# Self-attention of a four-layer kernel: where the causal mask of the transposed scores is applied, which engine splits q and k, and when constants are filled

## The reference

```python
K = jnp.einsum('bse,hed->bhsd', xk, Wk); V = jnp.einsum('bse,hed->bhsd', xv, Wv); Q = jnp.einsum('bqe,hed->bhqd', xq, Wq)
scores = jnp.einsum('bhqd,bhkd->bhqk', Q, K)
causal = jnp.triu(jnp.ones((xq.shape[1], sk), dtype=bool), k=1)
scores = jnp.where(causal, -jnp.inf, scores)
att = jax.nn.softmax(scores / jnp.sqrt(jnp.asarray(sk, scores.dtype)), axis=-1)
out = jnp.einsum('bhqk,bhkd->bhqd', att, V)
out = out.transpose(0, 2, 1, 3).reshape(out.shape[0], out.shape[2], -1)
return jax.nn.relu(out @ Wo + bo)
a = _layernorm(inputs + a, g1, b1)
```

## Time and profile before

| what | value |
|---|---|
| median of three runs | 3115.39 us |
| time of the profiled execution | 3107.04 us |
| its span, first to last instruction | 3105.3 us |
| mean granted TensorE clock | 0.898 of full speed |
| self_stage, first to last work | 1095.2 to 1972 us of the span |

### The profile page before, as it was taken

How to read it: one execution, slowest core, us unless ns; L and a number is a source line. 1 busy time by engine, 2 the same in 40 slices (tenths; PEclk the granted TensorE clock), 3 DMA queues, 4 the chain that set the end, 5 groups by cost and what they waited for, 6 DMA issues and landing times. The chain is left out here.

```text
span 3105.3 us, 44342 instructions
## 1 busy us (share of the span) xinstructions
PE 2582.5 (83%) x13167; PEld 1491.0 (48%) x13183; DVE 1717.8 (55%) x3471; ACT 1266.5 (41%) x2533; POOL 1165.0 (38%) x1679
## 2 busy tenths in 40 slices
PE   7997999999846658888988988699556887699997
PEld 4554666666523323343443433455333475466664
DVE  5884646555378736657556473488686734312211
ACT  4663435443345514555545556266211233122221
POOL 3666641344446630110201100144551062566663
PEclk9998999999968878999999999899657965799999
DMA  3001000001000031221312210110103061122222
GB/s 120 5 1 58 0 0 1 1 1 41 1 31 0 0 83 36 47 53 46 77 41 57 57 40 17 37 46 28 40 29 109 0 210 63 31 45 45 47 44 31
DMA packets 91525, 125.60 MB, mean 40 GB/s; under 512 B 14216, under 2 KB 68593, under 8 KB 89553
## 3 DMA queue, kind: packets, MB, share of 16 engines
q1 hardware_dynamic: 74416, 104.40, 11.4%
q0 software_dynamic: 16928, 18.93, 3.8%
HBM read 84.19 MB, written 38.83 MB: 40 GB/s over the span
## 5 line engine op out<-in xcount | busy, mean ns | idle before, releaser
L2558 ACT ACTIVATE L2S_pT<-L2S_t_ps 128x512 f32<-128x512 f32 (+3 forms) x768 | 353.8, 490 | 236.7 <-PE L2S_t_ps L2456 126.9
L2637 DVE TENSOR_REDUCE L2S_mx<-L2S_s_ps 128x1 f32<-128x768 f32 (+7 forms) x384 | 347.3, 953 | 110.7 <-PE L2S_s_ps L2435 107.6
L2453 PE MATMUL L2S_t_ps<-L2S_q,L2S_k 98*128 98x512 bf16 (+3 forms) x768 | 252.2, 342 | 40.6 <-ACT L2S_pT L2558 33.1
L2434 PE MATMUL L2S_s_ps<-L2S_k,L2S_q 96*128 96x512 bf16 (+3 forms) x768 | 208.5, 344 | 43.6 <-DVE L2S_mx L2637 32.6
L1034 POOL TENSOR_TENSOR L_prob<-L_prob,L_rc 128x616 f32<-128x616 f32 x128 | 156.7, 1225 | 205.8 <-DVE L_rc L980 205.5
L3092 DVE TENSOR_TENSOR L3B_h<-L3B_si,L3B_u_ps 128x512 f32<-128x512 f32 x71 | 48.9, 688 | 237.7 <-PE L3B_u_ps L3035 216.1
L2740 POOL DMA_DIRECT2D L2S_q<-L2S_mrow x32 | 17.3, 541 | 430.9 <-DVE L2S_mrow L2645 430.9
L2453 PEld LDWEIGHTS L2S_t_ps<-L2S_q,L2S_k 98*128 98x128 bf16 x768 | 75.6, 99 | 191.3 <-ACT L2S_pT L2558 147.4
L2471 PE MATMUL L2S_o_ps<-L2S_pT,L2S_v 128*32 128x512 f32 (+3 forms) x1536 | 166.8, 509 | 0.0
L571 POOL TENSOR_TENSOR L_prob<-L_prob,L_rc 128x616 f32<-128x616 f32 x64 | 77.8, 1215 | 234.9 <-DVE L_rc L524 234.9
L3009 POOL DMA_INDIRECT out<-L3B_y,L3F_rows x71 | 114.8, 1616 | 132.7 <-DVE L3B_y L3098 120.4
(11 more groups left out here) (451 smaller groups left out, 5928.2 us busy)
## 6 DMA issues: line engine op xcount, KB each, us to landing
qk_parts<-L2S_part SPq DMA_DIRECT2D x96, 128.0 KB, 2.3
L2S_q<-qk_parts SPq DMA_DIRECT2D x32, 192.0 KB, 3.4
L2S_k<-qk_parts SPq DMA_DIRECT2D x32, 192.0 KB, 3.5
L2S_q<-qk_parts SPq DMA_DIRECT2D x32, 128.0 KB, 3.2
L2S_k<-qk_parts SPq DMA_DIRECT2D x32, 128.0 KB, 3.2
self_attended<-L2S_att SPq DMA_DIRECT2D x4, 1024.0 KB, 4.2
L_xn<-self_attended SPq DMA_DIRECT2D x8, 512.0 KB, 3.6
context_attended<-L_res SPq DMA_DIRECT2D x8, 512.0 KB, 2.6
```

The source lines that it names most:

```text
L2434: nc.tensor.matmul(o[:, z * 512 + c:z * 512 + e], lhs, k6[0:KR, q % 2, h, c:e], start=True, stop=(e < end))
L2453: mm = nc.tensor.matmul(o[:, lo:512], k6[:, q % 2, j, kt * P:(kt + 1) * P], q6[:, q % 2, j, c * 512 + lo:(c + 1) * 512], start=True, stop= ...
L2558: nc.scalar.activation(pT[:, st % 2, j, lo:512], t_ps[j % 2][:, lo:512], ACT.Exp, scale=SK).then_inc(s["exp_done"], 1)
L2637: nc.vector.tensor_reduce(dst, src, AX.X, ALU.max).then_inc(s["mx_done"], 1)
```

## The change

Four edits, all in `self_stage`:

1. The matmul with `cmaskT` goes, with the tile itself. After the exponential of a diagonal unit POOL selects on the 128 x 128 corner of `pT`: what lies above the diagonal becomes 0 (`affine_select`, in place). `values` of a diagonal step waits for the four selections (`masked`). The mask of the peaks stays on PE.
2. DVE, and no longer POOL, makes the second and third part of q and k, right after the rest.
3. The ones in v are filled by DVE after the first layer norm's work.
4. The ones in `k6` are filled by POOL behind the constants. PE waits for them before its first instruction of the stage, and the next instruction of POOL waits as well.

```diff
+    DIAGONAL = [st for st, (c, kt) in enumerate(STEPS) if kt >= 4 * c]
...
-            pe.wait_ge(s["ones_done"], 1)
+            pe.wait_ge(s["k_ones"], 1)
...
                     o, lo = t_ps[j % 2], low(st)
-                    diagonal = kt >= 4 * c
-                    mm = nc.tensor.matmul(o[:, lo:512], k6[:, q % 2, j, kt * P:(kt + 1) * P], q6[:, q % 2, j, c * 512 + lo:(c + 1) * 512],
-                                          start=True, stop=not diagonal)
-                    if diagonal:
-                        mm = nc.tensor.matmul(o[:, lo:lo + P], identb[:], cmaskT[:], start=False, stop=True)
-                    mm.then_inc(s["t_full"], 1)
+                    nc.tensor.matmul(o[:, lo:512], k6[:, q % 2, j, kt * P:(kt + 1) * P], q6[:, q % 2, j, c * 512 + lo:(c + 1) * 512],
+                                     start=True, stop=True).then_inc(s["t_full"], 1)
...
                     pe.wait_ge(s["exp_done"], 4 * step + 4 + 2)
+                    if st in DIAGONAL:
+                        pe.wait_ge(s["masked"], 4 * (TB * (QUADS * b + q) + DIAGONAL.index(st) + 1))
...
-            nc.vector.memset(v[:], 1.0)
-            nc.vector.memset(k6[KR:MR], 1.0).then_inc(s["ones_done"], 1)
...
+                    if b is None:
+                        nc.vector.memset(v[:], 1.0).then_inc(s["ones_done"], 1)
...
                         dve.wait_ge(s["act_pre"], copies + 3 + 2 * m + f)
-                        dve.wait_ge(s["split_done"], 4 * nb + max(2 * m + f - 1, 0) + 1)
+                        n = 4 * nb + 2 * m + f + 1
+                        dve.wait_ge(s["split_done"], n)
                         nc.vector.tensor_tensor(rest[:, f, :], s_ps[f][:], part[:, f, 0, :], ALU.subtract).then_inc(s["rest_done"], 1)
+                        dve.wait_ge(s["rest_done"], n)
+
+                        if m or b is not None:
+                            dve.wait_ge(s[f"written{f}"], (2 * nb + m) * 96)
+                        nc.vector.tensor_copy(part[:, f, 1, :], rest[:, f, :]).then_inc(s["mid_done"], 1)
+                        dve.wait_ge(s["mid_done"], n)
+                        nc.vector.tensor_tensor(part[:, f, 2, :], rest[:, f, :], part[:, f, 1, :], ALU.subtract).then_inc(s["split_done"], 1)
...
-            nc.gpsimd.memset(cmaskT[:], 0.0)
...
-            pool.sem_inc(s["split_done"], 1)
-            first = 1
-            PER = 6
+            pool.wait_ge(s["const_done"], 1)
+            nc.gpsimd.memset(k6[KR:MR], 1.0).then_inc(s["k_ones"], 1)
+            pool.wait_ge(s["k_ones"], 1)
...
-                        nc.gpsimd.tensor_scalar(part[:, f, 1, :], rest[:, f, :], 1.0, None, ALU.mult).then_inc(s["pool_step"], 1)
-                        pool.wait_ge(s["pool_step"], own + 2 + 2 * m + f)
-                        nc.gpsimd.tensor_tensor(part[:, f, 2, :], rest[:, f, :], part[:, f, 1, :], ALU.subtract).then_inc(s["split_done"], 1)
+                def unit(q, st, j):
+                    if st in DIAGONAL:
+                        pool.wait_ge(s["exp_done"], ((QUADS * b + q) * NS + st) * 4 + j + 3)
                         chip.settle(pool)
+                        edge = pT[:, st % 2, j, low(st):low(st) + P]
+                        nc.gpsimd.affine_select(out=edge, in_=edge, compare_op=ALU.is_ge, fill=0.0, base=0,
+                                                pattern=[[1, P]], channel_multiplier=-1).then_inc(s["masked"], 1)
```

More of the change, by code:

```diff
@@ L2181, in self_stage @@
         xres = behind[:, 2 * S:].rearrange("p (t d) -> p t d", d=D)
-        cmask, cmaskT, identb = sb("cmask", [P, P], BF16), sb("cmaskT", [P, P], BF16), sb("identb", [P, P], BF16)
+        cmask, identb = sb("cmask", [P, P], BF16), sb("identb", [P, P], BF16)
         mx = sb("mx", [P, 2, 4, TB])
@@ L2588, in link @@
                 dve.wait_ge(s["dve_step"], step.up())
-            nc.vector.memset(v[:], 1.0)
-            nc.vector.memset(k6[KR:MR], 1.0).then_inc(s["ones_done"], 1)
             dve.sem_inc(s["mx_done"], 2)
+            dve.sem_inc(s["split_done"], 1)
             dve.sem_inc(s["r_free"], 1)
@@ L2700, in _ @@
             nc.gpsimd.affine_select(out=cmask[:], in_=cmask[:], compare_op=ALU.is_ge, fill=BIG, base=0,
-                                    pattern=[[-1, P]], channel_multiplier=1)
-            nc.gpsimd.affine_select(out=cmaskT[:], in_=cmaskT[:], compare_op=ALU.is_ge, fill=BIG, base=0,
-                                    pattern=[[1, P]], channel_multiplier=-1).then_inc(s["const_done"], 1)
-            pool.sem_inc(s["split_done"], 1)
+                                    pattern=[[-1, P]], channel_multiplier=1).then_inc(s["const_done"], 1)
+            pool.wait_ge(s["const_done"], 1)
+            nc.gpsimd.memset(k6[KR:MR], 1.0).then_inc(s["k_ones"], 1)
+            pool.wait_ge(s["k_ones"], 1)
             first = 1
-            PER = 6
+            PER = 2
             def batch(b, more):
                 nb = 0 if b is None else b + 1
-                own = first if b is None else first + 5 + PER * b
+                own = first if b is None else first + 1 + PER * b
                 R_AT = {("m", 0): 1} if b is None else uses_of_r(more)
@@ L2746, in batch @@
                 if b is None:
-                    before_all(norm=norm, project=project, turn_max=turn_max)
+                    before_all(norm=norm, turn_max=turn_max)
                 else:
-                    self_walk(more, turn_max=turn_max, norm=norm, project=project, finish=finish)
+                    self_walk(more, unit=unit, turn_max=turn_max, norm=norm, finish=finish)
             batch(None, True)
```

7 lines of the change are left out of this document (1 added, 6 removed).

## The result

The changed kernel takes 3123.18 us in the median of 20 runs (3116.76 to 3129.7), the kernel before 3116.77 us in 20 runs beside it (3109.27 to 3122.85). The ratio is 1.0023, with a 95% interval of 1.0014 to 1.0031: 4 to 10 us slower. Forecast were 3111 us, some 4.6 us less than before. The time lies in the range; the sign is wrong.

A forecast was written before the change was run, and what follows sets the result against it. PE leads, busy in 83% of the span, without being full. The terms, -6.9 - 3.1 - 13.6 + 9.8 + 9.2 = -4.6 us, gave 3111 us for the median; range 3098 to 3128 us.

The forecast's parts named there:

- terms 1 and 2: Prologue: moved fills let the norm go on earlier, -6.9 us; DVE makes the first split instead of POOL, -3.1 us.
- Term 3: Diagonal steps of the loop: masks leaving PE save 0.06 us for each on the path; -13.6 us.
- Rival A: Diagonal steps: the masks are worth their whole time on PE, 31 us, giving 3094 us; chance 0.20.
- Term 4: Quad 0 and the end of quad 3: `values` waits for POOL's selections behind `turn_max`; +9.8 us.
- The start of a batch hides its wait: Batch start: selections hold `values` of step 0 for 3.6 us, but PE waited until later before; no cost counted.
- rival C: Batch start: DVE's products block POOL's selections of steps 2 and 3; +5 us, 3116 us; chance 0.13.
- Term 5: Projects in the loop: DVE's split delays its first maximum, so PE stands 1.45 or 1.6 us each; +9.2 us.
- Rival D: Ends of quad 3 and behind projects: PE's clock falls to 1.2 GHz after new waits; up to +8 us; chance 0.09.
- slower, at 0.15: Whole kernel: slower than before by more than about 0.3%, 9.3 us; chance 0.15, against same 0.58 and faster 0.27.

The follow-up runs named there:

- e4: The kernel before without the mask matmuls of the transposed scores and with nothing in their place; ratio 0.9966 to the kernel before.
- e6: The changed kernel with the masks of steps 10 and 11 of every quad back on PE; ratio 0.9979 to the kernel before.
- e9: The changed kernel with the masks of steps 0 to 3 of quads 1 and 2 back on PE; ratio 1.0028 to the kernel before.
- e7: The changed kernel with DVE's last product and sum on a batch cut into pieces of 256 columns; ratio 0.9991 to the kernel before.
- e5: The changed kernel with the masks of quad 0's steps 0 to 3 back on PE; ratio 0.9994 to the kernel before.
- e2: The kernel before with DVE making the second and third part of q and k everywhere, masks still on PE; ratio 1.0036 to the kernel before.
- e10: The changed kernel with 8 unread products of constants on PE behind each project of the loop; ratio 1.0031 to the kernel before.
- e3: The kernel before with POOL's selections in place of the mask matmuls, POOL still splitting q and k; ratio 1.0167 to the kernel before.
- e1: The kernel before with the moved fills and DVE's split in the prologue only, its loop unchanged; ratio 0.9975 to the kernel before.
- e8: The kernel before with the prologue's changes, and selections only in steps 8 and 9 of every quad and 0 to 3 of quad 1; ratio 0.9929.
- e12: The changed kernel, masks of quad 0's steps 0 to 3 and all steps 10 and 11 on PE, 8 unread products behind each first project; ratio 0.9935.

## Why the prediction was wrong, step by step

**The prologue (terms 1 and 2) was right.** -10.0 forecast and measured; the root came 6.5 us earlier (6.9 said), the fill took 6.92, and from the first rest to the third part it took 2.0 us for 5.2 (3.2, said 3.1). That the sum agrees to the tenth is luck: the same edits gave 11.9 to 14.0 in the nine other kernels, where PE ran less at 1.2 GHz.

**Term 3 was perhaps a little too large**: 11.1 us for the masks (e4, one profile; 6.5 to 14.6 by the runs), not 13.6. Rival A (31) is excluded. The mechanism, short 0.06 us pieces of which a few a step are on the path, stood.

**Term 4 failed at one sentence: "The start of a batch hides its wait".** The waits it priced were there and smaller: 0.54 to 0.64 in quad 0 instead of 0.87, 0.93 for quad 3 instead of 1.83. The backlog runs at 0.25 us, not 0.32, which is all of it in quad 0 and 0.56 in quad 3; there the prediction also set all eight selections against 1362.3, where only step 10's `values` began, and step 11's came some 0.4 later. The start it left out cost 1.4, 2.1 and 0.7 us from the start of DVE's last sum to the next `mrow`, and the rows show three links. Two were cut by experiments: POOL's stop of 1.1 us (e6, e9; at batches 1 and 2 only), which the prediction didn't know, and selections held for the length of DVE's instruction (e7). The third, PE's order, by which the products of steps 2 and 3 and the first peaks stand behind `values` of step 1, is read from the rows; e5 takes all selections away from the start and shows only that without them the loss is gone. This is rival C, at steps 0 and 1 where it said 2 and 3 (1.5 to 2 us a start), at a chance of 0.13. The rule behind it (the Trainium skill, "SBUF — State Buffer", section "Who interferes with whom": a DVE instruction with two inputs in SBUF contends with a POOL instruction that reads SBUF, and the port pair that they share is an exclusive lock) agrees with the trace: 2.37 us for a selection beside 2.29 us of DVE, at most 1.15 once those are cut. DVE itself kept its 2.29.

**Term 5 was right in its direct part and lacked the clock.** DVE's first maximum came 1.44 and 1.33 us later, as forecast (1.6 and 1.45). But the first project's intervals cost 2.6 to 3.9 (e2), and are shorter again by 1.9 to 2.4 when PE is kept busy (e10); as the products also cover the first wait, which was there before, e10 shows what the clock is worth and not whose share is whose. The whole term is 12.6 against 9.2.

**The clock belonged into the sum.** Rival D said it would fall ahead of `make_v`; in the changed kernel's own profile it didn't (8.19 us as before), in e3, e9 and e10 it did in two batches of three. It fell behind the first project and, for 3.8 us, at the end of the last batch. Over the stage PE's time at 1.2 GHz went from 143 to 179 us. How much of the end's fall is the change's stays open: in e1, with none of the loop's edits, and in e8 and e12, where PE waits for no selection there, the transposes take 1.6 to 1.7 us more than before too. The products with Wo ran slow in the changed kernel and e10 alone.

Taken together the three loop terms measure -11.1 + 12.2 + 14.4 = +15.5 where the prediction had -13.6 + 9.8 + 9.2 = +5.4 (14.4 is e2's whole loop; 12.6 lie at the projects, and 1.6 in an interval that e1 shows longer as well). So the 10.1 us by which the loop missed lie at the starts of batches, in the clock behind the first project and at the last end, and in masks that were worth 2.5 less. The chances went wrong with it: slower, at 0.15, was what C, D and a slightly dearer term 5 make together, and the prediction never added its rivals up.

## What to carry to other kernels

An engine that was waiting is no cover for a new wait in its own queue: look at what stands between that wait and the work it waited for. When a queue is to take new work, list the long instructions of its neighbour engine beside it and those ahead of it in its own order; 192 selections with nothing near them cost nothing in e8, and all 512, behind POOL's own split, made the loop 52.5 us longer in e3. Price PE's waits with the clock that follows them, and add the rivals that share a sign.
